# A cross-attention and mixture-of-experts block on one core: from all eight experts for every token to the two chosen ones, by scattered rows

## Chip, core and metric

The kernel runs on one core of one Trainium2 chip. Its engines are TensorE (PE in the profile, with its weight loads as PEld), VectorE (DVE), ScalarE (ACT), GpSimd (POOL) and SyncE (SP, which here only issues DMAs). They run side by side and meet through semaphores. The metric is device time of one execution in microseconds, and lower is better. The kernel before took 327.93 us in the median of three runs (326.25 to 330.78).

## What is computed

There are 16 batches of 128 tokens with 128 features: 2048 tokens. A layer norm, a cross attention with 16 heads of 8 features and a residual come first. Then the part that the change is about:

```python
x = x + _L0_xattn_ref(_layernorm(x), ctx_1024, ctx_1024, mask, Wq, Wk, Wv, Wo)
x = x + _L0_ffn_ref(_layernorm(x), wg, w1, w3, w2)

# _L0_ffn_ref, E = 8 experts, I = 256 hidden features, TOP_K = 2
router_logits = x @ wg.T
probs = softmax(router_logits)
topk_w, topk_idx = top_k(probs, TOP_K)
topk_w = topk_w / sum(topk_w)
expert_w = sum(one_hot(topk_idx, E) * topk_w[..., None], axis=1)
h1 = einsum('th,eih->tei', x, w1)
h3 = einsum('th,eih->tei', x, w3)
y = einsum('tei,ehi->teh', silu(h1) * h3, w2)
out = einsum('te,teh->th', expert_w, y)
```

Only two of the eight weights in a row of `expert_w` are not zero.

## The kernel before

Everything is written out by hand, engine by engine, without a scheduler: the order in a block (`block.sync`, `block.tensor` and so on) is the order on that engine. Matrix products are made nearly exact by splitting each operand into a rounded part (`_hi`) and the rest (`_lo`) and adding three products (`split_product`, L431). ACT rounds a PSUM bank into `_hi`, DVE subtracts that from the bank into `_lo`.

**Attention.** The work goes in quarters `u` of four batches (512 tokens). Round `u` makes the scores of quarter `u` (L601, with the maxima on DVE, L1180) and, beside them, the second scores, exponentials and values of quarter `u - 1` (L584, L587, L562). Round 4 (`u == NQ`) therefore has only the last quarter's second half. Its ticks `NG * b + g`, 20 of them, also carry the start of the experts' part: the weights' transposes `("W", 0)` to `("W", 11)` in the order of `LAST_FILLS`, rounded by ACT and subtracted by DVE (L1075), the layer norm's statistics of finished quarters, and the routing of quarter 0.

**Routing.** `routing_step(q, 0..4)` on DVE compares each token's eight logits pairwise (L1035 to L1037), ranks them (L1040, L1041), selects the two best (`sel`, L1043) and forms the two weights with a tanh on ACT. The weights are transposed, written to HBM and read back broadcast over all partitions as `ewb`.

**Experts, before.** 64 units `n`: for each quarter of 512 tokens 16 blocks of 128 hidden features (8 experts x 256). A unit has nine matmuls over 512 columns: three for h1, three for h3 (L431) and, five units later (`LAG`), three for the down projection (L632), which sums all 16 blocks of a quarter in one bank. ACT does Silu (L819) and rounds the product (L660), POOL multiplies with the expert's weights (L897), DVE multiplies with h3 (L1205) and subtracts the rounded product (L1193). After a quarter its result is transposed (L437), added to `x_all` on DVE (L1064) and stored. No work depends on which experts were chosen.

`own(...)` on DVE makes an instruction wait for the end of the one before it. Work banks for transposes are handed around in the fixed order of `slot_order`; each fill of a bank waits until its last content is taken.

## Time and profile before

| what | value |
|---|---|
| median of three runs | 327.93 us (326.25 to 330.78) |
| profiled execution, its device time | 327.75 us |
| its span, first to last instruction | 325.9 us |
| PE busy | 280.9 us, 86% of the span |
| PEld busy | 209.9 us, 64% |
| DVE busy | 262.5 us, 81% |
| ACT busy | 176.2 us, 54% |
| POOL busy | 125.1 us, 38% |
| first matmul of expert unit 0 | 163.4 us after the span's start |

Busy time is the sum of what an engine's instructions took, as a share of the span. PE's ends are modelled and matmuls overlap, so PE's pace is better read from the distance between starts. The bracket at the end of a row of the timeline is the idle time before it, with the engine and line that ended it. A rising number of busy engines at once says that they overlap; which one sets the pace of a stretch must be read from the waits in that stretch.

### The profile page before, as it was taken

How to read it: one execution, taken by the hardware profiler on the slowest of the kernel's cores; microseconds unless marked ns; L12 is line 12 of the kernel's file. 1: busy time of each engine (PE TensorE's matmuls, PEld its weight loads, DVE VectorE, ACT ScalarE, POOL GpSimd, SP SyncE). 2: the span in 40 equal slices, each digit the busy share in tenths (PEclk: the TensorE clock that was granted, in tenths of full speed). 3: DMA queues.
4: the chain of work that ended last, by engine and by line, in shares of the span. 5: the costliest groups of instructions: out<-in, count | busy, mean ns of one | idle time of the engine just before them, and what ended most of it. 6: DMA issues, size and time to landing. Idle time of an engine off the chain costs nothing. (4 is left out here: it accounts for less than half of the span.)

```text
span 325.9 us, 5240 instructions
## 1 busy us (share of the span) xinstructions
PE 280.9 (86%) x1689; PEld 209.9 (64%) x1689; DVE 262.5 (81%) x523; ACT 176.2 (54%) x312; POOL 125.1 (38%) x111
## 2 busy tenths in 40 slices
PE   1947788989898989798899889897898978999994
PEld 0823565667566757575668667785686856888882
DVE  6586965887588757797649999879998799999893
ACT  6891256546655665375664355552455534666551
POOL 5201250125011501131166556554565535666660
PEclk9995599999999999999997999999999999999998
DMA  5984503340333043430800003400134001240101
GB/s 151 283 232 100 126 2 82 91 120 3 93 87 81 2 96 84 111 119 18 257 4 1 0 1 108 155 0 0 34 112 149 0 2 32 88 173 2 32 0 32
DMA packets 32618, 24.96 MB, mean 77 GB/s; under 512 B 2984, under 2 KB 27184, under 8 KB 32592
## 3 DMA queue, kind: packets, MB, share of 16 engines
q1 hardware_dynamic: 31440, 23.08, 25.1%
q0 software_dynamic: 320, 1.05, 1.3%
q10 hardware_dynamic: 832, 0.51, 0.6%
q8 instruction: 13, 0.21, 0.3%
q14 instruction: 13, 0.11, 0.1%
HBM read 15.12 MB, written 1.11 MB: 50 GB/s over the span
## 5 line engine op out<-in xcount | busy, mean ns | idle before, releaser
L897 POOL TENSOR_TENSOR big<-big,raw 128x512 f32<-128x512 f32 x64 | 87.9, 1375 | 70.3 <-ACT big L819 59.0
L431 PE MATMUL bank<-st,bd 128*128 128x512 f32 x320 | 88.9, 402 | 11.8 <-DVE big L1205 11.7
L431 PEld LDWEIGHTS bank<-st,bd 128*128 128x128 f32 x320 | 58.3, 190 | 28.5 <-DVE big L1205 17.5
L660 ACT ACTIVATE st<-big 128x512 fp32r<-128x512 f32 x64 | 40.5, 632 | 50.3 <-DVE big L1205 49.7
L1180 DVE TENSOR_REDUCE m_neg<-bank 128x4 f32<-128x512 f32 x64 | 43.2, 682 | 20.3 <-PE bank L601 20.0
L1205 DVE TENSOR_TENSOR big<-big,bank 128x512 f32<-128x512 f32 x64 | 43.5, 679 | 12.0 <-POOL big L897 11.7
L632 PE MATMUL bank<-st,bd 128*128 128x512 f32 x150 | 51.8, 397 | 0.2 <-DVE m_bd L1193 0.2
L819 ACT ACTIVATE big<-bank 128x512 f32<-128x512 f32 x64 | 38.0, 593 | 24.7 <-PE bank L431 24.3
L1193 DVE TENSOR_TENSOR m_bd<-big,st 128x512 fp32r<-128x512 f32 x42 | 47.4, 1129 | 0.1
L790 ACT ACTIVATE big<-bank 128x512 f32<-128x512 f32 x64 | 37.5, 600 | 17.4 <-PE bank L587 17.1
L601 PE MATMUL bank<-bd,st 128*128 128x512 f32 x64 | 30.1, 496 | 7.0 <-DMA bd<-st 6.6
L632 PEld LDWEIGHTS bank<-st,bd 128*128 128x128 f32 x150 | 28.5, 191 | 7.4 <-DVE m_bd L1193 0.9
L584 PE MATMUL bank<-m_bd,ones_b 128*128 128x512 f32 x64 | 29.4, 460 | 3.3 <-ACT big L790 1.9
L1120 DVE SCALAR_TENSOR_TENSOR st<-st_hi,cst,bank 128x512 fp32r<-128x512 f32 x32 | 23.4, 747 | 9.0 <-ACT st_hi L660 4.3
L855 POOL TENSOR_SCALAR ve<-mv 128x4 f32<-128x4 f32 x8 | 1.8, 229 | 69.2 <-DVE mv L925 69.2
L876 POOL TENSOR_TENSOR m_bd<-mT,cst 128x512 fp32r<-128x512 f32 x16 | 17.3, 1109 | 26.9 <-DVE mT L1093 26.9
L431 PE MATMUL bank<-st 128*128 128x512 f32 x64 | 25.3, 395 | 0.0
L587 PE MATMUL bank<-bd,st 128*128 128x512 f32 x64 | 25.3, 395 | 0.0
L601 PEld LDWEIGHTS bank<-bd,st 128*128 128x128 f32 x64 | 13.9, 221 | 14.0 <-issue 9.3
L1193 DVE TENSOR_TENSOR st<-big,st 128x512 fp32r<-128x512 f32 x22 | 22.5, 1023 | 0.0
L584 PEld LDWEIGHTS bank<-m_bd,ones_b 128*128 128x128 f32 x64 | 12.5, 195 | 10.4 <-issue 4.2
L562 PE MATMUL bank<-big 128*32 128x128 f32 x512 | 17.3, 276 | 0.0
(119 smaller groups left out, 422.5 us busy)
## 6 DMA issues: line engine op xcount, KB each, us to landing
bd<-st SPq DMA_DIRECT2D x128, 64.0 KB, 2.1
raw<-ew_rows SPq DMA_DIRECT2D x32, 256.0 KB, 5.0
x_all<-in_x SPq DMA_DIRECT2D x4, 256.0 KB, 3.9
mask_i<-in_mask_BxS_if POOLq DMA_DIRECT2D x4, 256.0 KB, 4.5
ctx_all<-in_L_ffn_w SPq DMA_DIRECT2D x1, 1024.0 KB, 5.8
out<-ck SPq DMA_DIRECT2D x4, 256.0 KB, 2.3
ctx_all<-in_ctx SPq DMA_DIRECT2D x3, 256.0 KB, 4.4
ctx_all<-in_ctx ACTq DMA_DIRECT2D x1, 256.0 KB, 5.5
```

The lines of the kernel that those rows point to most:

```text
L431: last = nc.tensor.matmul(o, w, m, start=(k == 0), stop=(k == len(pairs) - 1))
L584: nc.tensor.matmul(s2[k % 2][:, :], ones_b[:, b, :], m_bd[:, NJ * g:NJ * (g + 1), :].rearrange("p h q -> p (h q)"), start=True, stop=False)
L587: nc.tensor.matmul(s2[k % 2][:, :], st[:, (u - 1) % 2, 1, g, b * S:(b + 1) * S], bd_slot(0, n)[:, g, :, :].rearrange("p j q -> p (j q)"), ...
L601: nc.tensor.matmul(s1[k % s1_ring(u)][:, :], st[:, u % 2, 0, g, (b - 1) * S:b * S], bd_slot(1, n)[:, g, :, :].rearrange("p j q -> p (j q)" ...
L632: last = nc.tensor.matmul(yb[q % 2][:, :], w[2][:, k, :], g[n % RH], start=(k == 0 and c == 0), stop=(k == NB - 1 and c == 2))
L660: return nc.scalar.activation(o, i, ACT.Copy)
L790: nc.scalar.activation(prob[n % 2][:, NJ * g:NJ * (g + 1), :].rearrange("p h q -> p (h q)"), s2[k % 2][:, :], ACT.Exp, scale=SCALE).then_i ...
L819: nc.scalar.activation(sil[n % 3], h1[n % 2][:, :], ACT.Silu).then_inc(sil_ready, 1)
L897: nc.gpsimd.tensor_tensor(silw[n % 3], sil[n % 3], ewb[:, k // 2, :], ALU.mult).then_inc(silw_ready, 1)
L1180: nc.vector.tensor_reduce(m_neg[:, H * (b - 1) + NJ * g:H * (b - 1) + NJ * (g + 1)], s1[k % s1_ring(u)][:, :].rearrange("p (j q) -> p j q" ...
L1193: nc.vector.tensor_tensor(g_lo[n % RH], gg[n % 3], g_hi[n % RH].bitcast(F32), ALU.subtract).then_inc(glo_ready, 1)
L1205: nc.vector.tensor_tensor(gg[n % 3], silw[n % 3], h3[n % 2][:, :], ALU.mult).then_inc(gg_ready, 1)
```

## The change

The experts' part works on gathered rows. Each token is sent to its two experts, and only those products are computed.

- **Two phases.** Batches 0 to 11 (quarters 0 to 2) and batches 12 to 15 (quarter 3). Each phase has an HBM buffer `xg[f]` with a region per expert of `REGS[f]` rows (1664 and 640) of 129 numbers: the normalised token and, as the last number, its token number.
- **Routing.** For all four quarters DVE also keeps running counts per expert (`cum`), PE multiplies with a triangular matrix for each token's rank in its expert (`"rk"`), and `place_rows(q)` turns that into row numbers. The normalised rows are kept in SBUF (`rows2`, a ring of two quarters, each row twice). POOL sends them with 8 indirect DMAs per quarter (`send`), one per batch and choice. Quarters 0 to 2 are routed in round 4 of the attention (the first steps in round 3), quarter 3 between tiles.
- **Tables.** `table(f, ...)` computes on DVE which expert and which first row each tile of 128 rows has. The number of tiles is fixed by the worst case: `NTS` = 31 and 15, 46 in all. PE and SP load the numbers into registers. SP also writes rows of padding behind each expert's rows (`open_phase`: 9 DMAs per phase), and their token number is out of range, so that nothing is written for them.
- **Tiles.** For each of 46 tiles: SP loads 128 rows (a ring `xt` of `XR` = 8), PE transposes them, ACT rounds and DVE subtracts, PE makes h1 and h3 in one bank (two matmuls over 512 columns, two over 256), ACT Silu, DVE product, PE two transposes, ACT rounds and DVE subtracts, PE four matmuls over 256 columns, DVE adds the two halves of that bank (`take_rows`) into `y_sb` (a ring of 6), and POOL scatters the 128 result rows to `ys` in HBM by token number.
- **End.** SP loads all of `ys` (8 DMAs of 256 KB), and DVE adds both results, weighted, to `x_all`: 32 operations over 128 columns. Then four stores.
- The logits are now one float32 product with `wgT`, without the three-way split. The weights' products with POOL, the broadcast `ewb` and the per-quarter stores are gone.

```diff
+CT = 128
+PHASES = (3, NQ - 3)
+NTS = [(2 * c - E) // CT + E for c in CAPS]
+REGS = [c + CT for c in CAPS]
+XR, GR, YR = 8, 3, 6
...
+            def open_phase(f):
+
+                sp.wait_ge(pad_ready, f + 1)
+                sp.dma_start(xg[f][E * REGS[f]:E * REGS[f] + CT, :], consts[:, C_PAD:C_PAD + RW]).then_inc(padded[f], 16)
...
+                for row in at:
+                    sp.dma_start(xg[f][bass.ds(row, CT), :], consts[:, C_PAD:C_PAD + RW]).then_inc(padded[f], 16)
+                sp.wait_ge(tab_ready, f + 1)
...
+                for q in (range(3) if f == 0 else range(3, NQ)):
+                    sp.wait_ge(sent[q], 16 * 2 * QB)
+                sp.wait_ge(padded[f], 16 * (E + 1))
...
+            for n in range(NT):
+                f = int(n >= NTS[0])
+                if n == NTS[0] - XR + 1:
+                    rows += open_phase(1)
+                if n >= XR:
+                    sp.wait_ge(t_full, n - XR + 1)
+                    sp.wait_ge(ysb_out[(n - XR) % YR], 16 * ((n - XR) // YR + 1))
+                sp.dma_start(xt[n % XR], xg[f][bass.ds(rows[n], CT), :]).then_inc(in_t[n % XR], 16)
+            for k in range(YR):
+                sp.wait_ge(ysb_out[k], 16 * ((NT - 1 - k) // YR + 1))
...
+                nc.tensor.matmul(both, t_lo[n % 2], first_high[:, :, bass.ds(col[n], I)], start=True, stop=False)
+                nc.tensor.matmul(both, t_hi[n % 2], first_high[:, :, bass.ds(col[n], I)], start=False, stop=False)
+                for k in range(2):
+                    last = nc.tensor.matmul(h[:, k * I:(k + 1) * I], t_hi[n % 2], first_low[k][:, bass.ds(col[n], I)],
+                                            start=False, stop=(k == 1))
...
+                for c in range(2):
+                    w = second[:, :, bass.ds(col[n] + c * P, D)]
+                    nc.tensor.matmul(o, g_hi[n % GR][:, c * P:(c + 1) * P], w, start=(c == 0), stop=False)
+                    last = nc.tensor.matmul(o, g_lo[n % GR][:, c * P:(c + 1) * P], w, start=False, stop=(c == 1))
...
+            for n in range(NT + 3):
+                if n + 1 < NT:
+                    turn_tile(n + 1)
+                if n == NTS[0]:
+                    col += columns(1)
+                if n < NT:
+                    hidden(n)
+                if n >= 3:
+                    down(n - 3)
+                if 1 <= n < NT + 1:
+                    turn_hidden(n - 1)
...
+            for q in range(3):
+                pool.wait_ge(rows_ready, q + 1)
+                for m in range(2 * QB):
+                    send(QB * q + m // 2, m % 2)
...
+            for n in range(NT):
+                pool.wait_ge(ysb_ready, n + 1)
+                pool.wait_ge(in_t[n % XR], 16 * (n // XR + 1))
+                pool.indirect_dma_start(ys, bass.IndirectOffsetOnAxis(xt[n % XR][:, D:RW].bitcast(I32), 0), y_sb[n % YR], None,
+                                        bounds_check=PAIRS - 1, oob_is_err=False).then_inc(ysb_out[n % YR], 16)
...
+            def take_rows(n):
+
+                dve.wait_ge(down_done, n + 1)
+                if n >= YR:
+                    dve.wait_ge(ysb_out[n % YR], 16 * (n // YR))
+                ins = nc.vector.tensor_reduce(y_sb[n % YR], yb[:, 0:2 * D].rearrange("p (k d) -> p d k", k=2), X, ALU.add)
...
+                if n + 1 < NT:
+                    rest_of_tile(n + 1)
+                if n < NT:
+                    dve.wait_ge(sil_ready, n + 1)
...
+                if n >= 3:
+                    take_rows(n - 3)
+                if 1 <= n < NT + 1:
+                    rest_of_hidden(n - 1)
...
+                own(nc.vector.scalar_tensor_tensor(acc[b % 2], got[:, 0, b, :], wgt[:, b, 0:1], x_all[:, b, :], ALU.mult, ALU.add))
+                ins = nc.vector.scalar_tensor_tensor(o_sb[:, b, :], got[:, 1, b, :], wgt[:, b, 1:2], acc[b % 2], ALU.mult, ALU.add)
```

On ACT each step of the tile loop is: round tile n + 1, Silu of tile n, round the hidden part of tile n - 1.

Order on DVE, around the last weight subtractions (`bd <- bank,bd`, 512 wide) of round 4. Before, the heads of a batch (`rz`, `on`), its projection (`x_all`) and the subtractions are all that stands there:

```order
L989 TENSOR_TENSOR x_all<-bank,x_all 128x128
L1075 TENSOR_TENSOR bd<-bank,bd 128x512 x2
L995 RECIPROCAL rz<-bank 128x16
L998 TENSOR_TENSOR on<-bank,rz 128x128
L1075 TENSOR_TENSOR bd<-bank,bd 128x512
L989 TENSOR_TENSOR x_all<-bank,x_all 128x128
```

Now, at the same place, the row numbers of quarter 2 and the first part of the table stand between (`place`, `spread`, `rows_i`, then `pad`, `tiles`, `until`):

```order
L1235 TENSOR_TENSOR bd<-bank,bd 128x512
L1176 TENSOR_TENSOR place<-bank,cst 128x32
L1180 TENSOR_TENSOR spread<-place,which 128x64
L1182 TENSOR_REDUCE m_hl<-spread 128x8
L1183 CAST rows_i<-m_hl 128x8
L1206 COPY cnt<-bank 128x8
L1208 TENSOR_TENSOR pad<-cnt,cst 128x8
L1210 TENSOR_TENSOR cT<-cnt,cst 128x96
L1212 TENSOR_REDUCE tiles<-cT 128x8
L1213 TENSOR_TENSOR cT<-tiles,cst 128x64
L1214 TENSOR_REDUCE until<-cT 128x8
L1112 TENSOR_TENSOR x_all<-bank,x_all 128x128
```

What moved is that DVE passes ten small instructions before it takes the next projection `x_all`.

Order on PE in the experts' part. Before, one unit: the down projection of an older unit, then the six matmuls of h1 and h3.

```order
L632 MATMUL bank<-st,bd 128x512
L632 MATMUL bank<-m_bd,bd 128x512
L632 MATMUL bank<-st,bd 128x512
L431 MATMUL bank<-st,bd 128x512 x5
L431 MATMUL bank<-st 128x512
```

Now, one tile: `turn_tile(n + 1)` (L685), `hidden(n)` (L698 to L701), `down(n - 3)` (L722, L723), `turn_hidden(n - 1)` (L711). The ISA and REGISTER rows form addresses from the registers.

```order
L685 MATMUL bank<-cst,big 128x128
L698 ISA
L698 MATMUL bank<-bd,st 128x512
L699 MATMUL bank<-bd,st 128x512
L701 ISA
L701 MATMUL bank<-bd,st 128x256
L701 REGISTER_ALU
L701 MATMUL bank<-st 128x256
L722 ISA
L722 MATMUL bank<-bd,st 128x256
L723 MATMUL bank<-bd,st 128x256
L711 MATMUL bank<-cst,big 128x128 x2
```

The nine wide matmuls became eleven narrower ones, and `down` stands behind the `hidden` of a tile three later.

Order on SP in the middle of the tile loop: the loads of tiles 22 and 23 (`big <- xg`), then the opening of the second phase, whose rows of padding (`xg <- in_patterns`) stand ahead of the load of tile 24.

```order
L460 DMA big<-xg 128x129
L460 ISA
L460 DMA big<-xg 128x129
L438 DMA xg<-in_patterns 128x129
L439 TENSOR_LOAD pad
L442 ISA
L442 DMA xg<-in_patterns 128x129
```

Seven more such pairs of L442 follow, then `TENSOR_LOAD tab`. Before, SP at this time of the program issued only the eight broadcasts of the next quarter and a store.

## Rows read from the trace of the kernel before

**Rows 1.** Busy time by stretch: start:end, length, PE, PEld, DVE, ACT, POOL, PEclk, DMA share, GB/s.

```profile
0.00:20.00 20.00, 12.09 (x48) 9.59 (x48) 12.87 (x34) 15.04 (x20) 6.12 (x12) 1.00 0.83 232
131.50:163.40 31.90, 27.54 (x293) 20.07 (x294) 24.39 (x79) 18.66 (x41) 6.57 (x8) 1.00 0.43 125
131.50:159.00 27.50, 24.05 (x247) 17.51 (x247) 21.87 (x74) 15.64 (x34) 6.57 (x8) 1.00 0.39 107
163.40:321.00 157.60, 145.53 (x651) 114.80 (x650) 141.92 (x219) 80.75 (x139) 89.15 (x66) 0.99 0.14 46
```

**Rows 2.** Timeline of PE, one undisturbed expert unit: start, duration, engine, line, operation.

```profile
200.90 1.30 PE L431 MATMUL bank<-st,bd 128*128 128x512 f32 x5
...
202.94 0.84 PE L431 MATMUL bank<-st,bd 128*128 128x512 f32 x3
```

**Rows 3.** Timeline of PE: four transposes, then products with eight columns.

```profile
159.50 0.60 PE L437 MATMUL bank<-cst,ctx_all 128*128 128x128 f32 x4
...
172.10 0.25 PE L431 MATMUL bank<-wg_lo,st 128*128 128x8 f32 x1
172.21 0.36 PE L431 MATMUL bank<-wg_hi,st 128*128 128x8 f32 x2
```

**Rows 4.** Timeline of DVE in round 4: subtractions, pairwise comparisons, ranks, statistics, normalisation.

```profile
143.94 0.21 DVE L1035 TENSOR_TENSOR keep<-lg 128x64 f32<-128x64 f32 x1
...
145.11 0.43 DVE L1040 TENSOR_TENSOR keep<-keep 128x256 f32<-128x256 f32 x1
145.57 0.42 DVE L1041 TENSOR_REDUCE rank<-keep 128x32 f32<-128x256 f32 x1
146.03 0.69 DVE L1075 TENSOR_TENSOR st<-bank,bd 128x512 fp32r<-128x512 f32 x1
146.63 0.17 DVE L1043 TENSOR_SCALAR sel<-rank 128x32 f32<-128x32 f32 x1
146.84 0.19 DVE L1044 TENSOR_TENSOR ew<-sel,lg 128x32 f32<-128x32 f32 x1
...
147.99 0.86 DVE L920 BATCH_NORM_STATS2 stats<-x_all 128x6 f32<-128x128 f32 x4
148.89 0.38 DVE L925 BATCH_NORM_AGGREGATE mv<-stats 128x2 f32<-128x6 f32 x4
...
150.75 1.11 DVE L939 TENSOR_SCALAR xn<-x_all,mv,rstd 128x128 f32<-128x128 f32 x4
```

**Rows 5.** Timeline of ACT in round 4: copies out of PSUM, 256 and 128 wide.

```profile
160.21 0.39 ACT L660 ACTIVATE w_nat<-bank 128x256 f32<-128x256 f32 x1
...
162.83 0.28 ACT L660 ACTIVATE onT<-bank 128x128 f32<-128x128 f32 x1 [0.67 <-PE bank L457]
```

**Rows 6.** Line of the mask loads, which POOL issues: durations min/median/max in ns.

```profile
L846 POOL DMA_DIRECT2D mask_i<-in_mask_BxS_if x4: 622/628/762, 1.2 to 69.5; - x4
```

**Rows 7.** Page, DMA issues: out<-in, queue, count, KB each, median us to landing.

```profile
bd<-st SPq DMA_DIRECT2D x128, 64.0 KB, 2.1
...
out<-ck SPq DMA_DIRECT2D x4, 256.0 KB, 2.3
```

**Rows 8.** Timeline of SP: how long one issue holds it.

```profile
8.29 0.51 SPq L352 DMA_DIRECT2D x_all<-in_x  x1
```

**Rows 9.** Lines by form from 178 us on: POOL's product, and DVE's small operations beside it.

```profile
L897 POOL TENSOR_TENSOR big<-big,raw 128x512 f32<-128x512 f32 x58 | 79.6, 1372 | 59.9 <-ACT big L819 48.6 <-DVE big L1205 11.0
L1035 DVE TENSOR_TENSOR keep<-lg 128x64 f32<-128x64 f32 x12 | 6.6, 547 | 0.1
L1050 DVE TENSOR_SCALAR ew<-th 128x32 f32<-128x32 f32 x3 | 3.8, 1276 | 0.0
```

**Rows 10.** Busy time by stretch in the first scores, columns as in rows 1.

```profile
20.00:24.00 4.00, 0.30 (x1) 0.14 (x1) 3.33 (x7) 4.00 (x4) 0.00 (x0) 0.97 0.75 189
...
28.00:32.00 4.00, 3.77 (x7) 1.33 (x6) 4.00 (x13) 0.00 (x0) 1.27 (x2) 0.50 0.42 100
```

**Rows 11.** Chain that ended last, its last piece: start, duration, engine, tile, line.

```profile
322.52 0.69 DVE ck L1064
```

## Prediction before the run

> **What bounds the kernel now.** I read the stretches first [rows 1]. From 163.4 us to 321 us the experts' 64 units run: 157.6 us, 2.46 us each, PE busy for 145.5 us and DVE for 141.9 us. Then one unit on PE [rows 2]: from the start of one group of L431 at 200.90 to the next at 202.94 are nine matmuls in 2.04 us, 0.227 us each. So PE sets the pace, and DVE and POOL add the other 0.4 us in places. The reader should also see who is slack: in the last attention round, 131.5 to 163.4 us, DVE is busy for 24.4 of 31.9 us [rows 1], with 7.5 us free. That room is what the added routing falls into. The end is short: the last piece of the chain is a DVE addition at 322.52 [rows 11], then comes a store of 2.3 us [rows 7].
>
> **Removed.** All 64 units: the 157.6 us after 163.4 are replaced as a whole, so I build the new end from its parts. The trace shows the parts that repeat old operations. It shows no indirect DMA, no load of registers and no addressed matmul.
>
> **Prices.** DVE, one operand in PSUM: 512 columns take 0.69 us, and the next independent one starts 0.60 us after the start (146.03 to 146.63) [rows 4]. Between 256 columns (0.42) and 512 (0.69) lie 0.27 us, 1.05 ns a column [rows 4], so the step is 0.33 us for 256 and 0.20 us for 128. Small operations that wait for the one before cost 0.21 us a step (146.63 to 146.84), the comparisons of a batch 0.58 (143.94 to 145.11 holds two), the wide ones 0.46 (145.11 to 145.57) [rows 4]. ACT: 0.39 us for 256 columns, 0.28 for 128 [rows 5]. PE: 0.227 us for 512 columns [rows 2]; eight-column products start 0.11 us apart (172.10 and 172.21), which is the pace of the weight loads alone, and four transposes in 0.60 us fit the same step [rows 3]. A 256-column matmul lies between 0.11 and 0.227; half of 512 gives 0.12, which I take.
>
> **POOL's indirect DMA, c.** The nearest row is its direct DMA over 128 partitions: 0.63 us on the engine [rows 6]. That is the lower bound, since the indirect one also reads 128 indices. Above, the nearest is POOL's dearest operation, 1.37 us [rows 9], for want of anything that bounds it. I take 1.1 us, in the upper half because 128 separate addresses are more work than one pattern. Landing: 2.1 us for 64 KB between issue and arrival on SP [rows 7]; 1.9 us behind POOL's part. The Trainium skill, page "DMA: Bandwidth & Descriptors", section "Latency and other measured facts", puts the first byte of a POOL-issued DMA at about 1 us, for the emission. With that 1.0 in place of 1.1 the sum below would be 3 us lower.
>
> **1. Entry into the tile loop.** DVE gains, up to the last attention work: three routings in place of one. One is 0.22 + 4 x 0.58 + 2 x 0.46 + 0.22 for the old part to `sel`, 4 x 0.2 for `cum`, three small ones (0.6), two wide (0.92), two small (0.42): 6.4 us. Three are 19.2. Row numbers 3 x 0.95, weights 3 x 0.7, two normalisations of doubled width 2 x 1.75 (one old one is 1.11 us for four [rows 4]; 128 columns more in each add 0.13, the copy of ids and the gaps the rest), the table 4.3 (14 operations, four over 248 columns at 0.45). Total 32.0. Gone: one routing with its weights 4.8, one normalisation 1.1, the x2 splits 1.2, the weights' copy 0.7: 7.8. Net **+24.2 us**. Free are 7.5 us [rows 1], of which I let 4.5 be filled, since the rest waits on chains through PE and ACT. DVE's last attention work ends at 163.4 + 24.2 - 4.5 = 183.1.
>
> POOL is later. `rows_ready` of quarter 2 comes where DVE stood at about 159; up to there it gains 19.2 (without table and last weights) and fills 4.0 of 5.6 us free (27.5 less 21.87) [rows 1]: 174.2. Behind it queue eight sends (8.8), their landing (1.9), SP's load (2.1) and transpose, rounding and subtraction (1.0). First `hidden` at **188.0**, against 163.4 before.
>
> **2. One tile.** PE: 3 x 0.11 + 2 x 0.227 + 6 x 0.12 = 1.5 us. DVE: 0.20 + 3 x 0.33 = 1.2, with semaphore gaps 1.3. ACT below 1.1. POOL 1.1. None is the pace, I think. The ring of eight `xt` is. Load n + 8 waits for the scatter of tile n. `down(n)` stands behind `hidden(n + 3)`, and that behind the transpose of tile n + 4. So transpose n + 4 -> scatter n -> load n + 8 -> transpose n + 8 is a circle over four tiles. Its length: transpose and hidden 0.8, last matmul's way out 0.17, Silu 0.39, product 0.41, `take_rows` 0.41 (DVE does it only after the product; with results counted at their end, 0.41 for 256 columns): 2.2. POOL 1.1, scatter's landing 1.9, load 2.1, semaphores 0.1. Sum 7.4 us, **1.85 us per tile**.
>
> Iterations 0 to 8: DVE's 9 x 1.3 plus quarter 3's statistics, normalisation, routing and row numbers (1.25 + 1.75 + 6.4 + 0.95) = 22.1 us. Iterations 9 to 16: POOL has eight sends between eight scatters, 2 x 1.1 a tile: 17.6 (the table, 3.6, hides under it). Iterations 17 to 45: 29 x 1.85 = 53.7.
>
> **3. Opening phase 2.** SP does it with nothing loaded ahead. Nine issues of 0.51 [rows 8] are 4.6 us, the padding's landing 2.1, two register loads about 1 (an estimate; no row has one). One tile time, 1.85, hides: 6 us. PE's own load of registers at tile 31: 1 us.
>
> **4. The clock.** PE waited 5 us around 22 us, and its granted clock then was 0.50, the 1.2 GHz level, although PE was busy for 3.77 of 4.00 us between 28 and 32 [rows 10]. Entry and opening both leave PE idle for more than 4 us, and the first tiles behind run at half speed: 3 us together. In between, 1.5 us of work in 1.85 us should hold 2.4 GHz, as 27.5 busy of 31.9 us does [rows 1].
>
> **5. End.** Last tile from `hidden` to `take_rows` 3.6, scatter 1.1 + 1.9: 6.6. All results back: 2.1 MB at the 232 GB/s of the first 20 us [rows 1] is 9.0. The last quarter's eight weighted additions 2.2, the store 2.3 [rows 7].
>
> **Sum.** 188.0 + 22.1 + 17.6 + 53.7 + 6 + 1 + 3 + 6.6 + 9.0 + 2.2 + 2.3 = 311.5 us of span. The profiled execution took 327.75 with a span of 325.9, so 1.85 lie around it: **313 us**. Its 327.75 is within 0.2 us of the median 327.93, so no shift is needed.
>
> **Rivals.**
>
> *The ring is not the pace (faster still).* If scatter and load land 0.6 us sooner each, the circle is 6.2 us, and PE's 1.5 plus a gap, 1.55 us, sets the pace: -8.7. With c at its bound 0.65 (the circle then needs 0.35 us less of landing for that), entry -3.6, iterations 9 to 16 -5.2, and 2 us less of opening: 294. For it: 2.1 is a median that holds SP's own issue. Against: SP rings of 64 KB never land under 2.0 here.
>
> *DVE is held up beside POOL.* The comparison L1035 takes 0.21 us alone [rows 4] and 0.547 in the mean beside POOL's product, L1050 1.276 [rows 9]. If each of the 24 sends of the last round costs DVE 0.35 us, that is 8.4 us more at the entry, and the first nine tiles have no slack either: 322. Against: POOL's work for a DMA needn't use what its arithmetic uses. The Trainium skill, same page, section "SWDGE vs HWDGE vs iDMA", says that POOL writes descriptors into SBUF and that VectorE's two-port mode locks it out meanwhile. By that rule POOL is the one that waits, behind DVE's copies and tensor_scalars, which are few here; no row shows it.
>
> *POOL's indirect DMA is dear (slower).* Each microsecond on c costs 8 at the entry (the eight sends), 16 in iterations 9 to 16, 7.3 in the ring and 1 at the end: 32. The 14.5 us of gain are gone at c = 1.1 + 14.5 / 32 = 1.55 us. From c = 1.9 on POOL is the pace of the loop. At 2.2 (twice my value): +8.8 + 17.6 + 29 x 0.4 + 1.1 = 352. For it: POOL's plain product already needs 1.37 [rows 9], and one DMA has 128 addresses. Against: 0.63 for 128 partitions [rows 6].
>
> **Chances.** The forecast 0.48, the faster rival 0.16, DVE held up 0.17, POOL dear 0.19. The range leaves out the corner of the first and the upper part of the last: 294 to 336. About 2% can be told from no change, so faster means below 321.4: nearly all of the first two, 0.64. Within: most of the third, 0.16. Slower 0.20.
>
> **What would show it.** The first L698 near 188 us; if it comes near 175, the free time of DVE was larger or c smaller. The mean of the indirect DMAs on POOL: 1.1. From tile 17 on the distance of tiles should be 1.85 us with PE's transposes (L685) waiting for the DMA of `xt`. If they wait for DVE or never, the ring is not the pace. A gap of some 6 us before tile 24, with SP issuing L442. About 13.5 us from the last scatter's arrival to the end. The prediction is wrong as a whole if POOL is busy without a break in the loop, or if the attention's last round grew by much more than 20 us.

## The result and the profile after

| what | before | after |
|---|---|---|
| median | 328.31 us (4 runs, 326.25 to 330.78) | 342.01 us (4 runs, 341.02 to 346.11) |
| ratio after to before | | 1.039, 95% interval 1.0306 to 1.0474 |
| span of the profiled execution | 325.9 us | 344.5 us |
| PE, DVE, POOL busy | 280.9, 262.5, 125.1 us | 242.9, 228.6, 114.0 us |

The changed kernel is slower by 3.9%. The prediction said 313 us, with a range of 294 to 336. PE has 38 us less to do and DVE 34 us less, so the gain is there and was lost in waits. The profiled execution (346.11 us) is a slow one, the longest of the four, so the same kernel's later profiles stand beside it: run f1 (338.28 us, a span of 336.7) and run h2 (341.91 us, a span of 340.3).

The same stretches as [rows 1], each up to the moment when quarter 2's row numbers are ready (before: about 159 us), as busy time by stretch. First after's own trace, then run f1's:

```profile
131.50:186.39 54.89, 36.93 (x276) 28.59 (x273) 39.69 (x156) 18.11 (x39) 22.76 (x24) 0.72 0.18 54
```

```profile
131.50:183.52 52.02, 34.48 (x259) 26.43 (x259) 38.01 (x154) 16.65 (x37) 22.64 (x24) 0.71 0.19 55
```

DVE (third pair of busy columns) does 38.0 to 39.7 us of work against 21.9 before, and stands still for 14 to 15 us (12.9 in h2, below), where it stood still for 5.6 before. The granted clock is 0.71 to 0.72 where it was 1.00. DVE's longest wait in the stretch, in total us, times and longest us, is for PE's projection. First before (131.5 to 159), then f1 (131.5 to 183.52):

```profile
DVE x_all L989 <- PE bank L462: 3.8, 3, 1.5
```

```profile
DVE x_all L1112 <- PE bank L517: 7.3, 2, 3.7
```

POOL's two lines of indirect DMAs, minimum/median/maximum in ns:

```profile
L993 POOL DMA_INDIRECT xg<-rows,rows_i x32: 967/974/1252, 155.7 to 249.6; - x32
L1007 POOL DMA_INDIRECT ys<-big x46: 967/971/1079, 215.0 to 324.9; - x46
```

The chain that ended last, from POOL's last but one send to the first tile's first expert matmul (start, duration, what):

```profile
193.59 0.97 POOL xg L993
194.56 0.30 issue
194.87 0.97 POOL xg L993
195.84 0.30 issue
196.15 4.01 DMA xg<-rows,rows_i
...
200.41 1.87 DMA big<-xg
202.28 0.04 issue
202.32 0.49 PE bank L685
202.83 0.29 ACT st L766
203.14 0.30 DVE st L1376
203.45 0.13 issue
203.57 0.79 PE bank L698
```

A send holds POOL for 0.97 us and the next starts 1.28 us after it. The same chain, deep in the tile loop and at the end:

```profile
299.17 0.43 DVE big L1388
299.65 0.50 issue
300.36 2.56 DMA ys<-big
303.12 1.92 DMA big<-xg
305.41 0.36 PE bank L698
306.27 0.40 ACT big L930
307.03 0.43 DVE big L1388
307.51 0.50 issue
308.22 3.76 DMA ys<-big
...
324.87 2.10 DMA ys<-big
327.17 0.40 SPq L465
327.62 3.41 DMA raw<-ys
331.13 0.36 DVE big L1427
331.52 0.35 DVE ctx_all L1428
332.17 0.35 DVE ctx_all L1428
```

This is the circle of the prediction: scatter, load, tile, scatter. From 300.36 to 308.22 it takes 7.86 us, and its neighbours take 8.07 and 8.97 (scatters at 292.29 and 317.19), each for four tiles. The end is paced by DVE, with one batch each 0.65 us.

### The profile page after: what moved, and what is told of

Read it like the earlier page. It is cut to its first block, busy times and chain, and to the rows that moved or that the text cites. A ratio compares the mean times of both kernels' runs of the same rounds, so it can differ in the third digit from the quotient of the medians.

```text
span 344.5 us, 5853 instructions
## 1 busy us (share of the span) xinstructions
PE 242.9 (71%) x1591; PEld 184.6 (54%) x1591; DVE 228.6 (66%) x686; ACT 144.5 (42%) x318; POOL 114.0 (33%) x125
## 3 DMA queue, kind: packets, MB, share of 16 engines
q1 hardware_dynamic: 40208, 20.95, 24.9%
## 4 chain that ended last, share of the span: by engine, by line
PE 30%; DVE 23%; DMA 20%; issue 10%; SPq 10%; POOL 4%; ACT 3%; POOLq 0%; DVEq 0%; ACTq 0%
SPq L417 7%; DMA ys<-big 7%; PE bank L486 6%; DMA big<-xg 5%; PE bank L492 4%; DVE m_neg L1363 3%; DMA bd<-st 3%; PE bank L642 2%; PE bank L620 2%; PE bank L659 2%; PE bank L645 2%; PE bank L698 2%; POOL xg L993 2%; DVE ctx_all L1428 2%; DMA w_nat<-in_L_xattn_Wv 2%
## 5 line engine op out<-in xcount | busy, mean ns | idle before, releaser
L1007 POOL DMA_INDIRECT ys<-big x46 | 44.8, 974 | 61.6 <-DVE big L1388 53.8
L766 ACT ACTIVATE st<-bank 128x128 fp32r<-128x128 f32 (+1 forms) x92 | 28.3, 330 | 45.5 <-PE bank L685 25.6
L897 ACT ACTIVATE big<-bank 128x512 f32<-128x512 f32 x64 | 37.5, 597 | 23.4 <-PE bank L645 23.0
L993 POOL DMA_INDIRECT xg<-rows,rows_i x32 | 31.7, 992 | 22.2 <-DVE rows_i L1183 13.7
L1399 DVE TENSOR_TENSOR big<-big,bank 128x256 f32<-128x256 f32 x46 | 19.3, 420 | 22.9 <-ACT big L930 22.8
L685 PE MATMUL bank<-cst,big 128*128 128x128 f32 x46 | 15.3, 332 | 22.0 <-DMA big<-xg 21.7
L930 ACT ACTIVATE big<-bank 128x256 f32<-128x256 f32 x46 | 17.7, 385 | 31.0 <-PE bank L701 31.0
L698 PE MATMUL bank<-bd,st 128*128 x46 | 24.8, 539 | 5.5 <-DVE st L1376 3.8
L722 PE MATMUL bank<-bd,st 128*128 x92 | 27.3, 316 | 1.9 <-DVE big L1388 1.8
L723 PE MATMUL bank<-bd,st 128*128 x92 | 25.8, 299 | 0.0
L685 PEld LDWEIGHTS bank<-cst,big 128*128 128x128 f32 x46 | 7.4, 160 | 27.4 <-DMA big<-xg 27.3
L659 PEld LDWEIGHTS bank<-bd,st 128*128 128x128 f32 x64 | 14.2, 225 | 14.3 <-issue 9.3
L1381 DVE TENSOR_TENSOR st<-bank,st 128x256 fp32r<-128x256 f32 x46 | 19.5, 423 | 3.3 <-ACT st L766 2.8
L722 PEld LDWEIGHTS bank<-bd,st 128*128 128x128 f32 x92 | 18.9, 206 | 4.0 <-issue 3.4
```

The lines of the kernel that those rows point to most:

```text
L659: nc.tensor.matmul(s1[k % s1_ring(u)][:, :], st[:, u % 2, 0, g, (b - 1) * S:b * S], bd_slot(1, n)[:, g, :, :].rearrange("p j q -> p (j q)" ...
L698: nc.tensor.matmul(both, t_lo[n % 2], first_high[:, :, bass.ds(col[n], I)], start=True, stop=False)
L722: nc.tensor.matmul(o, g_hi[n % GR][:, c * P:(c + 1) * P], w, start=(c == 0), stop=False)
L723: last = nc.tensor.matmul(o, g_lo[n % GR][:, c * P:(c + 1) * P], w, start=False, stop=(c == 1))
L766: return nc.scalar.activation(o, i, ACT.Copy)
L897: nc.scalar.activation(prob[n % 2][:, NJ * g:NJ * (g + 1), :].rearrange("p h q -> p (h q)"), s2[k % 2][:, :], ACT.Exp, scale=SCALE).then_i ...
```

## The experiments

Each ratio is to the kernel before, measured side by side with the run. Runs e1 to e4, e5 to e7, e8, e9 to e11, f1 to f3, g1 and g2, and h1 and h2 are one set each. The diffs are shortened.

**e1 and e2: the ring.** One number changes:

```diff
-    XR, GR, YR = 8, 3, 6
+    XR, GR, YR = 7, 3, 6      # e1;  e2: 12, 3, 6
```

In both the opening of phase 2 stays at load 24.

> One size is changed: the ring of loaded tiles has 7 places, not 8. Theory ring (a circle of transpose, hidden, down, take_rows, scatter, load over XR - 4 tiles, which took 7.9 to 9.0 us in the changed kernel's chain): the circle now spans 3 tiles, 2.75 us each and not 2.05, over some 30 tiles, so 17 to 21 us slower than the changed kernel's 342, about 361. Rival (PE, DVE or POOL sets the pace of the loop and the loads are merely close): at most 3 us slower.

> One size is changed: the ring of loaded tiles has 12 places, and phase 2 is still opened ahead of load 24. Theory ring: the circle spans 8 tiles and no longer binds, tiles go at PE's and DVE's pace of 1.6 to 1.7 us, 11 us less over the loop, and the gap before tile 24 shrinks by 5 because 12 tiles are loaded ahead: about 326. No L685 waits for the load. Rival (another engine is the pace): 341, with the same distances of tiles.

Measured: 358.88 us with seven (1.0871, interval 1.0815 to 1.0927) and 324.65 us with twelve (0.9859, 0.98 to 0.9918). What PE's transposes of a tile (L685) waited for, in after, e1 and e2 (us, times; PE and its weight loads counted apart):

```profile
  DMA big<-xg: 48.9, 40
```

```profile
  DMA big<-xg: 79.5, 48
```

```profile
  DMA big<-xg: 18.6, 5
```

Late in the loop, eleven tiles without an interruption took 22.5 us with eight buffers (starts 293.2 and 315.7), 29.4 us with seven (299.3 and 328.7), and 17.6 us with twelve (276.0 and 293.6): 2.05, 2.67 and 1.60 us each. A circle of 8.2 us over XR - 4 tiles gives 2.05, 2.73 and 1.03. The last is below what PE needs, and there PE is busy in 23.77 of 25 us at a clock of 1.00. So the ring sets the pace at eight, and PE does at about 1.6 us with twelve.

**e3: the opening.** The padding of phase 2 is issued one DMA per load, at loads 16 to 24:

```diff
+                if n == 16:
+                    late = start_padding(1)
+                if 16 < n <= 16 + E:
+                    pad_expert(1, late[n - 17])
-                if n == NTS[0] - XR + 1:
-                    rows += open_phase(1)
+                if n == 16 + E + 1:
+                    rows += finish_phase(1)
```

> Ring of 8 as in the changed kernel. The nine padding writes of phase 2 are no longer issued in one piece ahead of load 24 but one before each of loads 16 to 24. Theory opening (SP's nine issues and their landing stand ahead of a load that has no slack): the 9.9 us between the hidden parts of tiles 22 and 23 fall to about 3, so 6 to 7 us less than 342, about 335. Rival (the pause only takes the place of ring waits that come later anyway): at most 2 us less.

Measured: 334.93 us (1.0138, 1.0064 to 1.0212). In after, SP does it all in one go:

```profile
257.17 0.33 SPq L460 DMA_DIRECT2D big<-xg  x1
257.55 0.54 SPq L438 DMA_DIRECT2D xg<-in_patterns  x1
258.95 5.78 SPq L442 DMA_DIRECT2D xg<-in_patterns  x8
267.13 2.04 SPq L460 DMA_DIRECT2D big<-xg  x4
```

From one load to the next are 9.96 us, and tile 23 starts 9.9 us after tile 22. In e3 that distance is 3.0 us (transposes at 257.53 and 260.57). The opening cost 7 us.

**e4: less ranking.** Quarters 1 and 2 skip comparison, ranking and choice (also in the later steps, which the cut doesn't show), and use quarter 0's choice, so their tokens go to other experts than the reference's:

```diff
+                if q in (1, 2) and k < 3:
+                    return
```

> Left out: for quarters 1 and 2 the comparison, ranking and choice; quarter 0's choice stands in, so the rows go to wrong experts, in the same number of DMAs and tiles. DVE has some 10 us less in the attention's last round. Theory serial (DVE's routing stands ahead of the heads in its order, PE waits for the heads and DVE later for PE, so idle time grows with the added work): more than 10 us less at the entry, the first hidden part at 190 or before, and DVE's idle time between 131.5 us and its last attention operation falls from 19.0 us by 3 or more. Rival DVE-bound: 10 us less, idle time unchanged. Rival POOL (its sends and their landing set the entry): less than 5 us.

Measured: 335.85 us (1.019, 1.0116 to 1.0265).

```profile
131.50:179.09 47.59, 33.29 (x276) 25.80 (x276) 30.73 (x118) 17.59 (x40) 21.87 (x24) 0.82 0.20 59
```

Beside e2 of the same set, whose row numbers came at 184.95 after 39.46 us of work, DVE has 8.7 us less to do and is ready 5.9 us earlier (4.9 and 5.7 beside e1 and e3). Its idle time grows from 14.0 to 16.9 us. The first L698 comes at 195.7, in e1 to e3 at 200.2 to 200.9. No theory has it whole. 'Serial' and 'DVE-bound' wanted 10 us, and 'serial' a shorter idle time. The gain of under 5 us is what the rival of the sends said, but POOL waits for DVE's row numbers before it sends. Some two thirds of the ranking's time are on the path, and in place of the rest DVE waits for PE, ACT and POOL.

**e5 and e6: the order.** In after, DVE's ranking stands ahead of a normalisation of heads for which PE waits 5.95 us (141.98) and 3.25 us (184.27). Behind it DVE waits 3.65 us for PE:

```profile
150.67 0.29 DVE L1112 TENSOR_TENSOR x_all<-bank,x_all 128x128 f32<-128x128 f32 x1 [3.65 <-PE bank L517]
```

e5 moves those two blocks behind it, and e6 quarter 1's too, with the products on PE and the tanh on ACT that belong to it. In short form, e5:

```diff
-    if u + 1 == NQ and (b, g) == (4, 0):  routing_step(0, 0); routing_step(0, 1)
-    if u + 1 == NQ and (b, g) == (4, 1):  routing_step(0, 2); routing_step(0, 3)
+    if u + 1 == NQ and (b, g) == (4, 2):  routing_step(0, 0); routing_step(0, 1)
+    # round 4, ahead of its first take_projection:  routing_step(0, 2); routing_step(0, 3)
-    if tick == 12:  routing_step(2, 2); routing_step(2, 3)
+    if tick == 13:  routing_step(2, 2); routing_step(2, 3)
```

> No work is added or taken away. Two of the blocks of ranking that stand in VectorE's order ahead of a normalisation of heads (L1118, L1121) are moved behind it: routing of quarter 0 from the start of tick (4,0) and (4,1) of round 3 to (4,2) and, its second half, to round 4 between the copy of the maxima and take_projection; the second half of quarter 2's from tick 12 to tick 13. In the changed kernel TensorE waits 5.95 us at 141.98 and 3.25 us at 184.27 for L1121, and VectorE then waits 3.65 us for TensorE before its next take_projection: the two engines stand still in turn. Theory 'order': the first L698 comes 4 to 8 us earlier (from 200 to 203.6 now to about 195), the whole kernel 335 us. Rival 'TensorE's clock and the sheer amount of work': the idle time of VectorE between 131.5 and its last attention operation (19.0 us) stays within 1.5 us, the first L698 within 2 us, the whole kernel 340 to 342 us.

> As the kernel with the reordered quarters 0 and 2, and quarter 1's too: the second half of its ranking goes from tick 5 to tick 10 (between the normalisation of heads and take_projection, where VectorE waits 3.60 us for TensorE at 176.46), its row numbers from tick 8 to tick 11, and what TensorE and ScalarE do for it follows. Quarter 1's sends start some 8 us later, when GpSimd has long finished quarter 0's. Theory 'order': 2 to 4 us better than the kernel that reorders quarters 0 and 2 alone, about 332 us. Rival 'the sends of the quarters form the path': not better or up to 4 us worse, since quarter 1's eight sends of 1.28 us then push quarter 2's (GpSimd waits in front of quarter 2's sends vanish).

Measured: 337.95 us (1.0267, 1.0207 to 1.0327) and 340.47 us (1.0357, 1.0291 to 1.0423). The fair comparison is e7 of the same set, which has after's order up to the tiles. First e5, then e7: the round's maxima (`m_hl`) and quarter 2's row numbers.

```profile
142.24 0.22 DVE L1130 TENSOR_TENSOR m_hl<-m_neg,m_hi 128x64 f32<-128x64 f32 x1
...
182.99 0.17 DVE L1183 CAST rows_i<-m_hl 128x8 int32<-128x8 f32 x1
```

```profile
145.47 0.22 DVE L1144 TENSOR_TENSOR m_hl<-m_neg,m_hi 128x64 f32<-128x64 f32 x1
...
183.06 0.17 DVE L1197 CAST rows_i<-m_hl 128x8 int32<-128x8 f32 x1
```

The maxima come 3.2 us earlier and the row numbers 0.07 us. The wait moved and the way didn't get shorter: the theory of the order, which wanted the first L698 4 to 8 us earlier, falls. It comes at 198.8 in e5, 198.9 in e7 and 199.0 in f1. What did change is what fills the time before the row numbers: DVE has 42.0 us of work and 9.7 us of idle time there, where e7 has 39.6 and 12.1. e5's median is 3 to 4 us below the changed kernel's in other sets, but the changed kernel was not measured beside it, and its span is f1's (336.9 and 336.7 us), so a gain from the order isn't shown. In e6 a new wait appears, 2.77 us of DVE for POOL's `rstd` behind the sends, and it is 2.5 us slower than e5, as its rival said.

**e7: the end.** The first twelve batches' results are fetched from load 40 on and added in the loop, and quarter 3's weights are formed at tile 13:

```diff
+                for b in range(2 * (n - 41), 2 * (n - 40)):
+                    if 0 <= b < 3 * QB:
+                        combine(b)
```

> The changed kernel, with the end of the first twelve batches' results taken into the loop: fetched from load 40 on, weighed and added two batches per iteration from tile 41 on, stored before the last scatter has landed; after the last tile only quarter 3's four batches remain. In the changed kernel the end from the last scatter's issue (324.87) to the end (344.5) is 19.6 us, of which 10.5 are 32 additions on VectorE. Theory: 12 of 16 batches at 0.65 us leave the end, minus what they delay in the loop, so 342 becomes 334 to 336. Rival 'VectorE is the bound of the last tiles': its 7.8 us reappear in tiles 41 to 45 (2.05 us each now) and the time stays at 340 or above.

Measured: 336.95 us (1.0217, 1.0135 to 1.0299), 4 to 5 us better than the changed kernel (340.74 to 342.01 in its sets without the pauses told of below), and just above the 334 to 336 of the theory. Beside f1's trace the end behind the last scatter's issue is 8.1 us shorter (11.5 for 19.6), and that scatter comes 5.2 us later (322.3 for 317.1): much of the work that left the end came back in the loop.

**e8 to e11: edits together.** e8 is e2, e3, e5 and e7 in one, with the early fetch at load 43 in one piece. e9, e10 and e11 are the ring of twelve with the order of e5, the opening of e3, and that early fetch.

> The changed kernel with four of the single edits together: ring of 12 token tiles (alone 342.0 to 324.7), the opening of phase 2 spread over the loads 16 to 25 (alone to 334.9; with the ring of 12 one opening is left of it, a gap of 7.7 us between the starts of tile 23 and 24 in that kernel's trace where the others take 1.6, so about 5 us), the results of the first twelve batches fetched at load 43 and added in the loop, two batches per iteration (alone to 337), and the two blocks of ranking moved behind the normalisation of heads (alone to 338). Theory 'each is its own place': 324.7 - 5 - 5 - 3 = about 312 us, the tiles at 1.6 to 1.7 us each from tile 10 on. Rival 'TensorE is the bound now and the edits overlap': with the ring of 12 TensorE is busy 95% of 270 to 295, the adds and the padding only move waits, and the time stays at 320 or above. In both cases below the kernel before (328.6).

Measured: 336.13 us (1.02, 1.0151 to 1.025), 24 us above the sum. ACT and DVE have pauses in this trace that end by nothing on this core ("remote").

> Ring of 12 token tiles and the two blocks of ranking behind the normalisation of heads. The kernel with four edits together took 336 where its single edits gave 312 by their sum; in its trace ScalarE starts bd at 165.44 after 4.24 us, and onT at 201.07 after 9.06 us, for nothing that the profile can name (an unknown queue), in the stretches in which GpSimd sends rows, and no other kernel's trace has such pauses. Theory 'the pauses come with the reordered ranking': they stand here too and the time is 330 or more. Rival 'they come with another edit': no such row, 324.7 - 3 = about 321.5.

> Ring of 12 and the opening of phase 2 spread over loads 16 to 25. Theory 'each edit is its own place': the gap of 7.7 us between tiles 23 and 24 of the kernel with the ring of 12 alone closes to some 2, and 324.7 becomes about 319. Rival 'the pauses without a named releaser come with this pair': rows on ScalarE or VectorE whose idle ends by an unknown queue, and 330 or more.

> Ring of 12 and the results of the first twelve batches fetched at load 43 and added in the loop (two batches per iteration from 40 on), only quarter 3's left for the end. Theory: the end after the last scatter loses 12 of 16 batches at 0.65 us, less what it delays in the loop, which is bound by TensorE here and not by VectorE: 324.7 becomes 318 to 320. Rival 'the pauses without a named releaser come with this pair': such rows, and 330 or more.

Measured: 334.86 us (1.0205, 1.0152 to 1.0258), 335.37 us (1.0211, 1.0141 to 1.0281) and 331.76 us (1.0109, 1.0068 to 1.0151), all three with such pauses. No edit could be blamed, since all were above the 324.65 of the ring alone, which had been measured in another set. So kernels were repeated, together.

**f1 to f3, g1 and g2: the same kernels again.** Nothing is edited. f1 and g1 are the changed kernel, f2 is e2, f3 and g2 are e8.

> The changed kernel itself once more, beside the kernels that are run with it on the same chip. If the pauses on ScalarE for which no releaser is named (9.1 us ahead of onT at 201 in the kernel with four edits) belong to the chip, they stand in this trace too and its time is 348 or more, where it was 342.0 before; if they belong to the kernels with a ring of 12 and a second edit, it is 340 to 343 and its trace has none.

> The ring of 12 alone once more, 324.65 on another chip. 'The pauses belong to the chip': here 330 to 335, with such rows around 165 and 190 to 200. 'They belong to the kernels that combine edits': 323 to 326, none.

> The four edits together once more, 336.1 on another chip. 'The pauses belong to the chip', and this chip is without them: 312 to 316. If this chip has them: 334 to 337 with the ring of 12 alone at 330 to 335 beside it. 'They belong to the kernel': 334 to 337 with the ring of 12 alone at 324.

Measured: 340.74 us (1.0394, 1.0307 to 1.0482), 322.96 us (0.9859, 0.9812 to 0.9906) and **312.22 us** (0.9537, 0.9496 to 0.9579), none with a pause. The very kernel that took 336 took 312 here, the time that the sum of its parts gave. The parts themselves differ from that sum. Between f2's trace and f3's (spans 321.1 and 310.3) the first L698 comes 1.2 us earlier where the order was to give 3, tiles 17 to 45 take 3.8 us less where the opening was to give 5, the end takes 6.4 us less where the early results were to give 5, and 0.6 us are lost in between. That the total fits so well is in part luck.

> The changed kernel a third time, beside the four edits together on the same chip. If this chip shows the pauses, the changed kernel has them too and takes 348 or more (its sends on GpSimd are the same 32), or, if only kernels with a ring of 12 have them, 340 to 343. If the chip shows none: 340 to 343.

> The four edits together a third time: 312 to 313 on a chip without the pauses (as on the last one), 334 to 337 on one with them (as on the first one). Nothing between is expected, if the pauses are the chip's.

Measured: 354.88 us (1.0769, 1.0692 to 1.0846) and 334.76 us (1.0173, 1.0102 to 1.0244), both with the pauses. So they belong to the set and not to the kernel, and the changed kernel has them too. Nor do they belong to one chip, as the expectations put it: f1 to f3 and g1 and g2 ran on the same one. The kernel before took 329.6, 328.5 and 329.0 us in the three sets with pauses, and 327.4 to 329.2 in the others: it is not touched. In g1's trace ACT does nothing while POOL sends rows:

```profile
194.03 0.60 ACT L766 ACTIVATE bd<-bank 128x512 fp32r<-128x512 f32 x1 [0.48 <-PE bank L492]
203.11 0.28 ACT L766 ACTIVATE onT<-bank 128x128 f32<-128x128 f32 x1 [8.48 <-remote]
```

```profile
190.61 0.97 POOL L993 DMA_INDIRECT xg<-rows,rows_i  x1 [9.60 <-DVE rows_i L1183]
...
199.56 0.97 POOL L993 DMA_INDIRECT xg<-rows,rows_i  x1 [0.30 <-issue]
```

In f1 the same `onT` waits 3.20 us, for PE. After's own trace has no row that ends by "remote", so its 342 us are the kernel's own.

**h1 and h2: TensorE's clock.** h1 adds matmuls that nothing reads, and h2 is the changed kernel beside it:

```diff
+                            if NG * b + g == 3:
+                                taken(pe, ("W", 4))
+                            if NG * b + g >= 3:
+                                for _ in range(3):
+                                    nc.tensor.matmul(bank[0][:, :], ones_b[:, 0, :], x_hi[:, :], start=True, stop=True)
```

> The changed kernel with 51 extra matmuls of 512 columns on TensorE in round 4 (three behind each tick from 3 on, into a bank that is free there; nothing reads them). At 0.227 us each they are 11.6 us of work on an engine that is busy for 22 of the 35 us between 165 and 200, at a granted clock of 0.72 to 0.76, where the kernel before had 1.00. Theory 'the low clock makes the way to the first tile long': the granted clock of 165:200 rises to 0.9 or more, the matmuls of the attention there halve, and the first L698 comes 3 to 6 us earlier although more work stands ahead of it; time 336 to 338 beside 341. Rival 'the chain over VectorE is what is long, and TensorE only waits': the extra work pushes the matmuls that VectorE waits for, the first L698 is the same or up to 6 us later, time 341 to 347.

> The changed kernel beside the one with the extra matmuls, as the measure of this call: 340 to 343, first L698 at 199 to 201; with the unnamed pauses of ScalarE 353 to 357 and 210.

Measured: 339.5 us (1.0354, 1.0296 to 1.0411) and 341.96 us (1.0424, 1.0372 to 1.0476). The intervals overlap. First h1, then h2, each up to quarter 2's row numbers and over 165:200:

```profile
131.50:184.14 52.64, 38.38 (x314) 30.16 (x303) 39.69 (x156) 18.11 (x39) 23.00 (x24) 0.88 0.20 56
165.00:200.00 35.00, 27.69 (x213) 21.59 (x211) 22.30 (x87) 12.55 (x27) 18.10 (x19) 0.89 0.24 58
```

```profile
131.50:184.43 52.93, 34.94 (x301) 26.37 (x294) 40.06 (x157) 17.84 (x40) 22.80 (x24) 0.80 0.20 57
165.00:200.00 35.00, 20.33 (x171) 14.60 (x171) 22.74 (x89) 11.44 (x25) 18.15 (x19) 0.77 0.23 56
```

PE's clock rises from 0.77 to 0.89, and the row numbers come at 184.1 instead of 184.4. The first L698 is at 202.07 against 200.86, 1.2 us later, so theory 'low clock', which wanted it 3 to 6 us earlier, isn't borne out. The 2.5 us by which h1's median is lower lie behind the entry, where the two kernels are the same (tiles 17 to 45 in 64.4 for 67.4 us). h1 can't tell what the faster clock gave from what the 51 matmuls cost. Traces that have the same entry and other clocks help: f1 at 0.71 has the row numbers at 183.5 and e7 at 0.80 has them at 183.2, and the ring of twelve has them at 184.95 with 0.71 (e2) and at 184.6 with 0.81 (f2). A tenth of the clock is not seen there. What a clock of 1.00 would give is not shown.

## Why the prediction was wrong, point by point

The sum of the prediction, 311.5 us of span, against three traces of the changed kernel (h2's execution is the one at its kernel's median):

| part | predicted | after | h2 | f1 |
|---|---|---|---|---|
| first L698 | 188.0 | 203.6 | 200.9 | 199.0 |
| iterations 0 to 8 | 22.1 | 25.5 | 25.5 | 24.3 |
| iterations 9 to 16 | 17.6 | 19.5 | 19.7 | 19.2 |
| iterations 17 to 45 with opening, columns and clock | 63.7 | 70.9 | 69.4 | 69.4 |
| from there to the end | 20.1 | 25.1 | 24.9 | 24.9 |
| span | 311.5 | 344.5 | 340.3 | 336.7 |

Tile times are the starts of L698 in PE's timeline. The last of them, tile 45's, is 317.38 in after, and its iteration is counted with 2.05 us. The miss in iterations 0 to 8 (2.2 to 3.4 us) has no run of its own. Part of it is the half clock, which the prediction had counted in the fourth row.

1. **Entry, the step that failed.** It is the largest miss, 11.0 to 15.6 us. The added work of DVE was right. Up to quarter 2's row numbers I had put 19.2 us of it, gaps included, on top of 21.87. In f1 it is 16.1 us of busy time and 2.3 us more of the short gaps between instructions (3.1 for 0.8), 18.4 in all. Wrong was "fills 4.0 of 5.6 us free". The free time was not filled. DVE's waits for other engines grew from 4.8 to 10.9 us, 3.5 us of it in the wait for the projection (3.8 to 7.3 above), and the row numbers came at 183.5 (f1) or 186.4 instead of 174.2: 10.1 us of waits too few, 0.8 us of work too much. I treated idle time as a store to be used up. It is made of waits for engines that in turn wait for DVE, and in after PE stands still for 5.95 and 3.25 us for DVE's `on`. Part of such time can be filled (e5 has 2.4 us more work in it and is ready at the same moment), but an added block is not free: e4 took 8.7 us of blocks away and got 5.9 us back. What made the waits longer stays open. Not the ranking alone, since without two quarters of it DVE idles longer (16.9 us). Not the place of two of its blocks (e5). A clock of 0.81 in place of 0.71 changes nothing that can be seen, and 1.00 was not tried.

   Behind the row numbers 13.8 us were predicted, and it took 15.5 (f1), 16.4 (h2) and 17.2 (after). In f1 nearly all of the rest is the eight sends, 10.7 us for 8.8.

2. **POOL's indirect DMA.** Taken was c = 1.1 us. Measured is 0.97 us of work and 0.30 us of issue: 1.28 us from one to the next. By the prediction's own prices this is 0.18 us for each of 8 DMAs at the entry and 16 in iterations 9 to 16, where sends and scatters follow one another without a pause: 1.4 and 2.9 us. The rival "dear" needed 1.55. Its chance, 0.19, was most of what "slower" had, so "slower" came by another way than the one it was priced for. In iterations 9 to 16 POOL sets the pace only through the ring: f2 has the same sends, and with twelve buffers these iterations take 16.0 us there for 19.2 in f1. The Trainium skill, page "DMA: Bandwidth & Descriptors", section "Latency and other measured facts", puts the first byte of a POOL-issued DMA at about 1 us, for the emission. POOL's busy time of 0.97 us fits that, but what the sum needed was the distance of two sends.

3. **The ring is the pace.** Right, and e1 and e2 show it from both sides. The mis-sized term is the circle: 7.4 us predicted, 7.9 to 9.0 measured. From the end of `take_rows` to the scatter's landing I had 3.0 us, and the chain shows 0.76 us of semaphore and issue (307.46 to 308.22) and then 2.56 to 3.76 us. That is 2.05 us a tile for 1.85, and 6 us over 29 tiles.

4. **Opening phase 2.** 6 us predicted. The gap is 9.9 us, less one tile's 2.05, so 7.9 us, and e3 gave 7 us back. The eight issues to register addresses follow one another at 0.72 us (5.78 for eight) where I had 0.51. PE's own load of registers at tile 31 was put at 1 us: tile 31 starts 3.6 us after tile 30 in f1, about 1.5 us more than one tile.

5. **DVE held up beside POOL.** Refuted. A comparison beside the sends takes 0.22 us, as alone [rows 4], where [rows 9] had 0.547 beside POOL's product. In g1, with its pauses, it takes 0.22 too: they stand between instructions and are no slower work.

6. **The clock.** In the tiles behind the entry and the opening it was half, as predicted: 0.50 in f1 from 199.0 to 203.0 and from 263.8 to 266.6 us. It was lower in the whole last round as well, at 0.71 to 0.80, which I had not foreseen. No run gives its price.

7. **The end.** Taken was that the results' 2.1 MB need 9.0 us and DVE adds 2.2. Measured: the first results are there 4.0 us after the load starts, and then DVE needs 0.65 us for each of 16 batches, 10.4 us. DVE is the bound and the transfer hides: 14.4 us for 11.2. From the last scatter's arrival to the end it is 17.5 us, where I had named 13.5 as a sign.

Terms 1, 2, 3, 4 and 7 are all too low. Term 1 took added work as covered by idle time, and term 7 took a transfer as the bound where the work on DVE stood in the path. The gain of the forecast was 14.5 us, and the errors sum to 25 (f1), 29 (h2) and 33 (after). With the ring, the opening and the end mended the kernel takes 312.22 us (f3, which has e5's order too), below both. That this is near the forecast's 313 is chance: it is another kernel, and its entry is 11 us longer than the forecast's. The entry is as long there as in the changed kernel: its first tile matmul starts at 198.9.

## What to carry to other kernels

Free time of an engine is a safe store only if its work is independent. In a round where four engines answer each other, count an added block as a lengthening of the chain unless you can name the wait that it runs beside: here two thirds of the ranking's time counted. A ring whose load waits for a late consumer has the pace (circle's length) / (buffers - tiles inside the pipeline). Work it out with one more and one fewer buffer, since a longer ring is the cheapest repair: here four more buffers brought 17.8 us side by side (340.74 to 322.96, f1 and f2). Dispatching only the chosen tokens took 38 us of work from PE, and the time went to what comes around it, the padding, the row numbers, the sends and the collecting.

## What the runs showed of the hardware

- An indirect DMA of 128 rows of 516 or 512 bytes holds POOL for 0.97 us (0.967 to 1.25), a waiting one follows 0.30 us later, and it lands 2.3 (scatters) or 2.7 us (sends) after its start in f1's median. In after the send on the chain at the entry took 4.01 us, and the longest took 5.3.
- In three of the seven sets of experiments (e8; e9 to e11; g1 and g2) ACT and DVE had pauses of up to 9 us without a releaser on the core, in the stretches where POOL sent rows (154 to 200 and about 235 to 265 us in g1). They go with 14 us more for the changed kernel (354.88 for 340.74) and 22.5 us more for f3's kernel (334.76 for 312.22). The kernel before, without indirect DMAs, had the same time in all sets. What differs between the sets isn't in the traces. The pauses and the sends coincide in time, and no run shows that one causes the other.
- Reading registers from SBUF seems to take time on SP: between the first padding's issue, which ends at 258.09, and the second at 258.95 lie 0.9 us, with one such read in them. From the last padding's issue (264.73) to the next load 2.4 us pass, with the table's read and the padding's landing in them. The rows do not part them.
